# Low passes one image later, weight preparation over images 21 to 31, and a rearranged last stage

## The chip, the cores and the metric

The kernel runs on one NeuronCore of one Trainium2 chip. The time is device microseconds of one execution; the time before is the median of three runs. One further execution was profiled. Engines are named as the profile names them: PE (TensorE matmul; PEld its weight load), DVE (VectorE), ACT (ScalarE), POOL (GpSimd), SP (SyncE, which only issues DMAs here).

## The reference

Input x is 32 images of 128 channels and 32x32 pixels, float32.

```python
x = x + L0(_gn(x))     # _gn: group norm over 32 groups of 4 channels
x = x + L1(_gn(x))
# L0: xs = conv(x, w_i2s * mask, 1x3) + b_i2s       (taps 0 and 1 only, tap 1 masked)
#     for each of the 32 rows of an image:
#         hc = conv(h, w_s2s, 1x3 along the 1024 columns b*w) + b_s2s
#         i, f, g, o = split((x_row + hc) @ w_ih.T + b_ih + b_hh)
#         c = sigmoid(f) * c + sigmoid(i) * tanh(g);  h = sigmoid(o) * tanh(c)
# L1: y = conv(x, W * het_mask, 3x3, p=4) + sum(b, axis=1)
#     het_mask: all nine taps where (i - n) % 4 == 0, the centre tap elsewhere
```

## The kernel before

The program has three stages, one behind the other. Within a stage every engine runs a fixed list of instructions, written out in Python in the order in which they are issued, and semaphores tie the engines together. An instruction that waits holds back all that stands behind it on its engine.

**First stage: the input convolution, one image b = 0 to 31 per loop turn ("step b").** ACT normalizes the image (`norm_image`, L914, writes `xn`) and rounds it to float16 (`high_image`, L924, writes `hi`; for every fourth image, b % 4 == 0, POOL does this, L825). POOL forms the remainder `lo` (L827). PE then does for the image eight **high** matmuls (`input_high`, `wi_hi` and `wi_lo` on `hi`, two halves of the image) and four **low** matmuls (`input_low`, `wi_hi` on `lo`; the last one raises `xconv_done`). An image's result lies in PSUM until it is copied into `img` by `store_xs`: ACT does even images (L929) and DVE odd ones (L601), both two steps late (`EVAC_LAG = 2`), so ACT's store of image b-2 stands in its list behind the norm and the rounding of image b. Three images fit in PSUM and three in each of `xn`, `hi` and `lo`.

The group norm needs statistics. DVE takes them (`bn_stats`, L466, two instructions for an image), sums a chunk of up to four images (`bn_aggr`, L474), and a chain of small steps follows: PE `sum_means`, DVE `chain_mean`, PE `sum_vars`, DVE `chain_var`, ACT `square_root`, DVE `chain_rstd` (ends with `nbias`, L511). `CHAIN_AT` and `ROOT_AT` say at which step PE, DVE and ACT do their part. The sums for images 18 to 21 are at step 14, for 22 to 25 at step 18, for 26 to 29 at step 22 and for 30 and 31 at step 26; their roots are on ACT at steps 16, 20, 24 and 28, behind the norm of that step and ahead of its store.

In the same stage the weights are prepared: PE turns them by transposes (`turn` with `raw_s` and `raw_g`, `turn_conv` with `turn_c`), all three into one PSUM bank, and DVE splits each result into a high and a low half (`split`, L575 and L578; `split_conv`, L589 and L596). Since they share the bank, the next turn waits until the split before it is done (`split_done`). DVE's `top_weights` and `scale_weights` find the scale of the last convolution's weights, and one DVE instruction of 1152 columns (L648) scales them for all three rows of taps. `TURN_STATE`, `TURN_GATES`, `TURN_ROWS`, `TOP_AT`, `SCALE_AT` and `TURN_CONV_AT` name the steps.

**Second stage: the recurrence,** 96 items (32 rows times 3 column blocks); nothing of it is changed.

**Third stage: the last convolution, 16 groups g of two images.** ACT writes the normalized images into `pad` (L1016), DVE their low parts (`lo`, L729). Four classes of output channels q = 0 to 3 need different input channels, so POOL copies every `pad` twice into a `stack` (L883 for odd classes, L884 for even ones) and then shifts the even classes' rows (L888, two instructions); the odd ones' are shifted by two DMAs from SP (`stack_below`, L415). PE does for a group `dense` (L1249) and `tiled` (L1271) for each of three `TERMS`, then `residual` (L1259), then `above_and_below` (L1291, 144 matmuls that read the stacks), whose last matmul raises `conv_done`. ACT and DVE then finish two classes each (`finish_class`, L1035 and L735), and SP stores the group by four DMAs of 256 KB; of the last group's four, ACT issues two.

Of the kernel before, what the change touches and what calls it, by code (L numbers as in the profile page):

```python
# [19 lines left out]
Q = 4  # L20
# [64 lines left out]
ACT_CLASSES, DVE_CLASSES = (0, 2), (1, 3)  # L85

# [30 lines left out]
def build_network(nc, x, w_i2s, b_i2s, w_s2s, b_s2s, w_ih, b_ih, b_hh, w_conv, b_conv, consts, out):  # L117
# [4 lines left out]
    with ExitStack() as ctx:  # L122
# [138 lines left out]
        conv_done = sem("conv_done")  # L261
        class_set = sem("class_set")
# [109 lines left out]

        @block.sync
        def _(sp):
# [59 lines left out]
            for g in range(GROUPS):  # L434
                sp.wait_ge(out_act, len(ACT_CLASSES) * (g + 1))
                sp.wait_ge(out_dve, len(DVE_CLASSES) * (g + 1))
                store_group(sp, g, range(Q) if g < GROUPS - 1 else range(2))
                for b in range(PAIR * (g + 2), min(PAIR * (g + 3), B)):
                    stack_below(b)
            sp.wait_ge(stored, 16 * Q * GROUPS)  # L440
# [3 lines left out]
        def _(v):  # L444
# [140 lines left out]

            def split_conv(d):
# [35 lines left out]
            for b in range(B):  # L622
# [16 lines left out]
                if b == TURN_STATE + 1:  # L639
                    split(1, ws_hi, ws_lo)  # L640
# [6 lines left out]
                if b == TURN_CONV_AT:  # L647
                    v.tensor_scalar(turn_c[:].rearrange("p k (q n) -> p k q n", q=Q),  # L648
                                    raw_c[:].rearrange("p (n q) k -> p k q n", q=Q), scl[:, 5:6], None,
                                    ALU.mult).then_inc(raws_ready, 1)  # L650
                if b - 1 in TURN_ROWS:
                    split_conv(TURN_ROWS.index(b - 1))
            zlow(0)
# [77 lines left out]

            def finish_class(g, q):

                v.wait_ge(conv_done, g + 1)
# [34 lines left out]
            lo(2)  # L769
            image_stats_again(2 * CH - 1)  # L770
            bn_aggr(FIRST_CHUNKS + 2)
            lo(3)
            chain_mean(FIRST_CHUNKS + 2)
            image_stats_again(HELD)
            image_stats_again(HELD + 1)
            for g in range(GROUPS):
# [3 lines left out]
                finish_class(g, DVE_CLASSES[0])  # L780
                if chain:
                    chain_mean(FIRST_CHUNKS + k + 1)
                finish_class(g, DVE_CLASSES[1])
# [7 lines left out]
                if near < B:  # L791
                    lo(near)
                if chain:
                    chain_rstd(FIRST_CHUNKS + k + 1, (k + 1) % 2)
# [4 lines left out]
                if near < B:  # L799
                    lo(near + 1)  # L800

        @block.gpsimd
        def _(pool):
# [70 lines left out]
            for b in range(PAIR, B):  # L874
# [10 lines left out]
                pool.wait_ge(odd_stacked, b - PAIR + 1)  # L885
# [5 lines left out]
        def _(act):  # L891
# [40 lines left out]
            for q in QUARTERS[2:]:  # L932
                load_quarter(act, 0, q)
# [423 lines left out]
```

## Time and profile before

| what | value |
|---|---|
| median of three runs | 638.57 us (636.14 to 638.76) |
| the profiled execution's own time | 636.83 us |
| its span | 635.0 us |
| busy | PE 92%, DVE 80%, ACT 76%, POOL 64% |
| first stage | 0 to about 124 us |
| second stage | about 124 to 434 us |
| third stage | about 434 to 635 us |
| TensorE clock granted, whole run | 0.984 of full |

A busy share is an average over three stages with different limits. For this change only the first and the third stage are read: in each, the question is which wait of PE ends last, and what the engine that is waited for was doing before. A matmul's duration in the rows is modelled and overlaps the next one, so PE's pace is read from the distance between two starts.

### The profile page before, as it was taken

How to read it: one execution, taken by the hardware profiler on the slowest of the kernel's cores; microseconds unless marked ns; L12 is line 12 of the kernel's file. 1: busy time of each engine (PE TensorE's matmuls, PEld its weight loads, DVE VectorE, ACT ScalarE, POOL GpSimd, SP SyncE). 2: the span in 40 equal slices, each digit the busy share in tenths (PEclk: the TensorE clock that was granted, in tenths of full speed). 3: DMA queues.
4: the chain of work that ended last, by engine and by line, in shares of the span. 5: the costliest groups of instructions: out<-in, count | busy, mean ns of one | idle time of the engine just before them, and what ended most of it. 6: DMA issues, size and time to landing. Idle time of an engine off the chain costs nothing.

```text
span 635.0 us, 19609 instructions
## 1 busy us (share of the span) xinstructions
PE 581.3 (92%) x7741; PEld 382.4 (60%) x7741; DVE 507.3 (80%) x1187; ACT 485.8 (76%) x867; POOL 403.7 (64%) x373
## 2 busy tenths in 40 slices
PE   0889897999999999999999999995799999999995
PEld 0434444578888888878888888883444444343342
DVE  4887887489999999999999999997876786666430
ACT  1678884899999999989999999997373645536440
POOL 1478885545555555565555555554479999998891
PEclk9999997999999999999999999997899999999999
DMA  9978940004314444224443144400156465664745
GB/s 242 273 221 269 232 53 1 3 4 68 51 29 57 67 68 66 41 28 67 68 68 51 26 60 66 68 2 1 26 133 167 122 164 133 151 159 118 178 121 150
DMA packets 89659, 61.47 MB, mean 97 GB/s; under 512 B 73952, under 2 KB 75232, under 8 KB 89568
## 3 DMA queue, kind: packets, MB, share of 16 engines
q1 hardware_dynamic: 88608, 58.90, 44.4%
q10 hardware_dynamic: 960, 1.31, 0.7%
q8 instruction: 62, 1.02, 0.7%
q14 instruction: 29, 0.24, 0.1%
HBM read 35.07 MB, written 16.78 MB: 82 GB/s over the span
## 4 chain that ended last, share of the span: by engine, by line
PE 61%; POOL 17%; DVE 10%; ACT 5%; issue 4%; DMA 1%; SPq 0%; POOLq 0%; DVEq 0%; ACTq 0%
PE ps L1191 18%; PE ps L1169 13%; PE ps L1196 9%; POOL stack L888 8%; PE ps L1173 6%; POOL stack L884 5%; POOL stack L883 4%; PE ps L1291 3%; PE ps L1114 3%; PE ps L1115 3%; DVE bn L466 3%; PE ps L1249 2%; PE ps L1271 1%; ACT xn L914 1%; DMA img<-in_x_dram 1%
## 5 line engine op out<-in xcount | busy, mean ns | idle before, releaser
L846 POOL TENSOR_TENSOR fc<-gate,cell 128x352 f32<-128x352 f32 (+16 forms) x96 | 83.8, 873 | 141.6 <-ACT gate L975 141.6
L1191 PE MATMUL ps<-z_hi,wg_hi 128*128 128x352 f32 (+13 forms) x384 | 134.3, 351 | 1.2 <-ACT z_hi L959 0.8
L1191 PE MATMUL ps<-z_hi,wg_lo 128*128 128x352 f32 (+13 forms) x384 | 122.0, 319 | 0.0
L1196 PE MATMUL ps<-z_lo,wg_hi 128*128 128x352 f32 (+13 forms) x384 | 107.5, 320 | 0.0
L975 ACT ACTIVATE gate<-ps,gate_bias 128x352 f32<-128x352 f32 (+16 forms) x192 | 104.2, 543 | 2.9 <-PE ps L1196 2.9
L975 ACT ACTIVATE ps<-ps,gate_bias 128x352 f32<-128x352 f32 (+16 forms) x192 | 99.5, 518 | 0.0
L856 POOL TENSOR_TENSOR img<-hT,xr 128x352 f32<-128x352 f32 (+1 forms) x96 | 88.7, 924 | 5.8 <-DVE hT L693 5.6
L1035 ACT ACTIVATE img<-ps,finish 128x512 f32<-128x512 f32 x32 | 23.2, 774 | 89.1 <-PE ps L1291 81.0
L827 POOL TENSOR_TENSOR lo<-xn,hi 128x1024 f16<-128x1024 f32 x32 | 68.1, 2131 | 28.4 <-ACT hi L924 27.2
L466 DVE BATCH_NORM_STATS2 bn<-img 128x6 f32<-128x512 f32 x120 | 75.8, 681 | 7.6 <-DMA img<-in_x_dram 7.5
L1191 PEld LDWEIGHTS ps<-z_hi,wg_hi 128*128 128x128 f32 x384 | 72.3, 188 | 8.1 <-ACT z_hi L959 1.4
L1191 PEld LDWEIGHTS ps<-z_hi,wg_lo 128*128 128x128 f32 x384 | 72.5, 189 | 0.0
L1196 PEld LDWEIGHTS ps<-z_lo,wg_hi 128*128 128x128 f32 x384 | 68.2, 188 | 0.8 <-DVE z_lo L607 0.3
L888 POOL COPY stack<-pad 32x1074 f32<-32x1074 f32 x46 | 60.0, 1304 | 4.6 <-POOL stack L884 0.4
L672 DVE TENSOR_TENSOR hrow<-ps,tc 128x352 f32<-128x352 f32 (+16 forms) x96 | 49.2, 513 | 16.9 <-ACT tc L984 15.7
L735 DVE TENSOR_SCALAR img<-ps,finish 128x512 f32<-128x512 f32 x32 | 25.0, 806 | 45.5 <-PE ps L1291 44.9
L607 DVE SCALAR_TENSOR_TENSOR z_lo<-ps,z_unscale,z_hi 128x352 fp32r<-128x352 f32 (+15 forms) x96 | 54.9, 572 | 3.8 <-ACT z_hi L959 2.4
L1169 PE MATMUL ps<-hh,ws_hi 128*128 128x352 f16 (+19 forms) x279 | 56.7, 312 | 0.5 <-DVE hh L679 0.5
L1173 PE MATMUL ps<-hl,ws_hi 128*128 128x352 f16 (+19 forms) x279 | 55.7, 308 | 0.4 <-DVE hl L685 0.4
L1169 PE MATMUL ps<-hh,ws_lo 128*128 128x352 f16 (+19 forms) x279 | 55.7, 308 | 0.0
L1291 PE MATMUL ps<-stack,wk_hi 64*32 64x512 f16 x1440 | 47.8, 383 | 7.8 <-POOL stack L888 4.3
L959 ACT ACTIVATE z_hi<-ps,z_unscale 128x352 fp32r<-128x352 f32 (+15 forms) x96 | 52.4, 546 | 0.2
(141 smaller groups left out, 1309.8 us busy)
## 6 DMA issues: line engine op xcount, KB each, us to landing
xr<-in_x_dram SPq DMA_DIRECT2D x64, 256.0 KB, 5.5
img<-in_x_dram SPq DMA_DIRECT2D x126, 128.0 KB, 3.8
out_dram<-img SPq DMA_DIRECT2D x62, 256.0 KB, 4.2
stack<-pad SPq DMA_DIRECT2D x46, 134.2 KB, 2.5
stack<-pad_first SPq DMA_DIRECT2D x14, 134.2 KB, 3.0
raw_c<-in_L_conv_W_dram SPq DMA_DIRECT2D x4, 144.0 KB, 2.6
out_dram<-img ACTq DMA_DIRECT2D x2, 256.0 KB, 4.6
img<-in_x_dram ACTq DMA_DIRECT2D x2, 128.0 KB, 3.4
```

Source lines behind the costliest of these rows:

```text
L466: v.bn_stats(bn[:, j, s, :], src[:, 512 * s:512 * s + 512]).then_inc(bn_done, 1)
L607: v.scalar_tensor_tensor(out=z_lo[it % 2][:, 0:n], in0=z_even(it), scalar=z_unscale[:], in1=z_hi[it % 2][:, 0:n].bitcast(F32), op0=ALU.mul ...
L827: pool.tensor_tensor(lo0[slot][:], xn0[slot][:], hi0[slot][:], ALU.subtract).then_inc(lo0_done, 1)
L846: pool.tensor_tensor(fc[it % 2][:, 0:c1 - c0], gate[it % 2][0][:, 0:c1 - c0], cell[:, c0:c1], ALU.mult).then_inc(fc_done, 1)
L856: pool.tensor_tensor(img32[:, b0:b1, t, :], hT[it % 2][:, 0:W * (b1 - b0)].rearrange("p (b w) -> p b w", w=W), xr[:, r % 2, b0:b1, t % 2, ...
L888: pool.tensor_copy(below(b, q).bitcast(F32), rows_below(b, q).bitcast(F32)).then_inc(even_below, 1)
L975: act.activation(gate[it % 2][m][:, 0:n] if m in (0, 2) else gate_columns(it, m), gate_columns(it, m), ACT.Tanh if gt == G_GATE else ACT.S ...
L1169: pe.matmul(z, w[:, tap, :], hh[u][:, c0 + tap:c1 + tap], start=False, stop=False, skip_group_check=True)
L1173: ins = pe.matmul(z, ws_hi[:, tap, :], hl[u][:, c0 + tap:c1 + tap], start=False, stop=(tap == 2), skip_group_check=True)
L1191: pe.matmul(gbank(it, m)[:, 0:n], w[:, GATE_ORDER[m], :], z_hi[it % 2][:, 0:n], start=(w is wg_hi), stop=False)
L1196: pe.matmul(gbank(it, m)[:, 0:n], wg_hi[:, GATE_ORDER[m], :], z_lo[it % 2][:, 0:n], start=False, stop=True).then_inc(gate_ready, 1)
L1291: ins = pe.matmul(rows(out_rows(g, 2 * half + k, c)), WK[w][r, k, e], pixels.rearrange("p (h w) -> p h w", w=PADW)[:, :, 0:W], start=False ...
```

## The change

1. **First stage, low passes.** At step b PE does the high passes of image b and then the low passes of image b-1. Step 0 has no low passes, step 31 has those of images 30 and 31. `xconv_done` of an image is thus raised one step later in PE's list; no other engine's list is moved for that.
2. **First stage, weights.** The turn of `raw_s` goes from step 0 to step 21, its split from step 1 to step 23; the turn of `raw_g` from 22 to 23, its split from 23 to 24; `top_weights` from 22 and 23 to 25 and 26; `scale_weights` from 24 to 27. The single DVE instruction of 1152 columns becomes three of 384, at the ends of steps 28, 29 and 30 (`turn_row`), and `turn_conv` on PE goes from steps 26, 28, 30 to 28, 29, 30, each waiting for its own `turn_row`.
3. **Start.** ACT loads its function table (the `Sqrt` on `warm`) before it issues the DMAs of `raw_i`, `raw_s`, `mask` and `ident`, not behind them.
4. **Third stage, copies.** The copy of `pad` for the odd classes goes from POOL to DVE (`stack_odds`), behind each `lo`.
5. **Third stage, order on PE.** In groups 1 to 14 the residual and the stack matmuls of the first two terms come before the dense and tiled matmuls of the third term; only the third term's stack matmuls stay last.
6. **Last group.** The stack matmuls of the even classes come first and raise `evens_done`; each of ACT and DVE finishes one even class, then one odd class; the stores are split in even and odd classes of 128 KB, eight DMAs in all, of which six lie on SP and two on ACT.

```diff
-TURN_STATE, TURN_GATES, TURN_ROWS = 0, 22, (26, 28, 30)
+TURN_STATE, TURN_GATES, TURN_ROWS = 21, 23, (28, 29, 30)
-BIAS_AT, TOP_AT, SCALE_AT, TURN_CONV_AT = 16, (22, 23), 24, 25
+BIAS_AT, TOP_AT, SCALE_AT = 16, (25, 26), 27
...
+            def turn_row(d):
+                k = slice(3 * d, 3 * d + 3)
+                v.tensor_scalar(turn_c[:, k].rearrange("p k (q n) -> p k q n", q=Q),
+                                raw_c[:].rearrange("p (n q) k -> p k q n", q=Q)[:, k], scl[:, 5:6], None,
+                                ALU.mult).then_inc(raws_ready, 1)
...
-                if b == TURN_STATE + 1:
+                if b == TURN_STATE + EVAC_LAG:
                     split(1, ws_hi, ws_lo)
...
-                if b == TURN_CONV_AT:
-                    v.tensor_scalar(turn_c[:]...
                 if b - 1 in TURN_ROWS:
                     split_conv(TURN_ROWS.index(b - 1))
+                if b in TURN_ROWS:
+                    turn_row(TURN_ROWS.index(b))
...
+            def stack_odds(b):
+                v.wait_ge(lo_done, b + 1)
+                if b >= PAIR + SLOTS:
+                    v.wait_ge(conv_done, (b - SLOTS) // PAIR + 1)
+                v.tensor_copy(stack[b % SLOTS][1][:].bitcast(F32), pad[b % SLOTS][:].bitcast(F32)).then_inc(odd_stacked, 1)
...
-                evens, odds = stack[b % SLOTS]
-                pool.tensor_copy(odds[:].bitcast(F32), pad[b % SLOTS][:].bitcast(F32)).then_inc(odd_stacked, 1)
-                pool.tensor_copy(evens[:].bitcast(F32), pad[b % SLOTS][:].bitcast(F32)).then_inc(even_stacked, 1)
+                pool.tensor_copy(stack[b % SLOTS][0][:].bitcast(F32), pad[b % SLOTS][:].bitcast(F32)).then_inc(even_stacked, 1)
...
-                pe.wait_ge(raws_ready, 3)
+                pe.wait_ge(raws_ready, 3 + d)
...
                 input_high(b, 1)
-                input_low(b)
+                if b > 0:
+                    input_low(b - 1)
+                if b == B - 1:
+                    input_low(b)
...
+                if g < GROUPS - 1:
+                    residual(g)
+                    stacks_ready(g)
+                    above_and_below(g, TERMS[:2], (0, 1), False)
+                    dense(g, TERMS[2:], False)
+                    tiled(g, TERMS[2:], SIDES, False)
+                    above_and_below(g, TERMS[2:], (0, 1), True).then_inc(conv_done, 1)
+                else:
+                    dense(g, TERMS[2:], False)
+                    tiled(g, TERMS[2:], SIDES, False)
+                    residual(g)
+                    stacks_ready(g)
+                    above_and_below(g, TERMS, (0,), True).then_inc(evens_done, 1)
+                    above_and_below(g, TERMS, (1,), True).then_inc(conv_done, 1)
```

How the order moves on PE around step 22. `hi00`, `lo00` are the slots of image 21 (21 % 3 = 0), `hi01`, `lo01` those of image 22, `hi02` that of image 23 (and 20). Before, from the low passes of image 21 on:

```order
L1114 MATMUL ps<-lo00,wi_hi 128x512 [waits lo0_done]
L1115 MATMUL ps<-lo00,wi_hi 128x16x31
L1114 MATMUL ps<-lo00,wi_hi 128x512
L1115 MATMUL ps<-lo00,wi_hi 128x16x31
L1082 MATMUL ps<-mv,group_mean 128x4 [waits aggr_done]
L1091 MATMUL ps<-ident,raw_g 128x128 [waits split_done,par_in]
L1091 MATMUL ps<-ident,raw_g 128x128 x3
L1114 MATMUL ps<-hi01,wi_hi 128x512 [waits xs_odd_done,hi0_done]
```

And now, from the second half of image 22's high passes on:

```order
L1149 MATMUL ps<-hi01,wi_hi 128x512 [waits xs_odd_done,hi0_done]
L1150 MATMUL ps<-hi01,wi_hi 128x16x31
L1149 MATMUL ps<-hi01,wi_lo 128x512
L1150 MATMUL ps<-hi01,wi_lo 128x16x31
L1149 MATMUL ps<-lo00,wi_hi 128x512 [waits lo0_done]
L1150 MATMUL ps<-lo00,wi_hi 128x16x31
L1149 MATMUL ps<-lo00,wi_hi 128x512
L1150 MATMUL ps<-lo00,wi_hi 128x16x31
L1126 MATMUL ps<-ident,raw_g 128x128 [waits split_done,par_in]
L1126 MATMUL ps<-ident,raw_g 128x128 x3
L1149 MATMUL ps<-hi02,wi_hi 128x512 [waits xs_even_done,hi0_done]
```

The low passes of image 21 are now the last thing ahead of the turn of `raw_g`, and this turn waits for `split_done` of `raw_s`.

DVE at the same place, now: the end of the chain of step 22, the store of image 21, statistics of image 31, and the splits.

```order
L526 SCALAR_TENSOR_TENSOR nbias0<-ps,rstd0 128x4 [waits gn_step]
L623 COPY img<-ps 128x1024 [waits xconv_done]
L481 BN_STATS bn<-img 128x6 [waits x_in7]
L481 BN_STATS bn<-img 128x6
L590 CAST ws_hi<-ps 128x384 [waits prep_T]
L593 TENSOR_TENSOR ws_lo<-ps,ws_hi 128x384 [waits prep_hi]
L598 COPY wgT<-ps 128x512 [waits prep_T]
```

The split of `raw_s` (`ws_hi`, `ws_lo`) stood some 170 rows further up before, at step 1; now it stands behind a store that waits for the low passes of image 21.

POOL in the third stage, one image before:

```order
L883 COPY stack21<-pad2 128x1107
L884 COPY stack20<-pad2 128x1107
L888 COPY stack20<-pad2 32x1074 x2
```

and now:

```order
L917 COPY stack30<-pad3 128x1107
L920 COPY stack30<-pad3 32x1074 x2
```

The full copy for the odd classes has left POOL; DVE has it behind its `lo`.

## Rows read from the trace of the kernel before

**Rows 1.** Ten microseconds: length, busy (instructions) of PE, PEld, DVE, ACT, POOL; clock, DMA

```profile
100.00:110.00 10.00, 6.54 (x24) 4.29 (x25) 5.62 (x18) 1.45 (x3) 5.24 (x3) 0.66 0.01 2
```

**Rows 2.** Timeline, PE: start, length, engine, line, instruction, [idle before <-releaser]

```profile
96.68 0.38 PE L1114 MATMUL ps<-hi,wi_hi 128*128 128x512 f16 x1
...
99.05 0.38 PE L1115 MATMUL ps<-lo,wi_hi 128*128 128x496 f16 x1
101.72 0.38 PE L1082 MATMUL ps<-mv,group_mean 128*128 128x2 f32 x2 [2.29 <-DVE mv L474]
103.85 0.90 PE L1099 MATMUL ps<-ident,turn_c 128*128 128x128 f32 x3 [1.75 <-DVE turn_c L648]
...
106.49 0.63 PE L1115 MATMUL ps<-hi,wi_hi 128*128 128x496 f16 x1
106.92 0.63 PE L1114 MATMUL ps<-hi,wi_lo 128*128 128x512 f16 x1
...
124.23 0.38 PE L1115 MATMUL ps<-lo,wi_hi 128*128 128x496 f16 x1
```

**Rows 3.** Timeline, ACT in the first stage: images 10 to 14, and 22

```profile
49.95 1.24 ACT L914 ACTIVATE xn<-img,nbias,rstd 128x1024 f32<-128x1024 f32 x1 [1.12 <-DVE nbias L511]
...
54.35 1.06 ACT L924 ACTIVATE hi<-xn 128x1024 f16<-128x1024 f32 x1
55.32 1.23 ACT L914 ACTIVATE xn<-img,nbias,rstd 128x1024 f32<-128x1024 f32 x1
56.45 1.00 ACT L929 ACTIVATE img<-ps 128x1024 f32<-128x1024 f32 x1
...
61.05 1.24 ACT L914 ACTIVATE xn<-img,nbias,rstd 128x1024 f32<-128x1024 f32 x1 [1.12 <-DVE nbias L511]
...
83.57 1.23 ACT L914 ACTIVATE xn<-img,nbias,rstd 128x1024 f32<-128x1024 f32 x1
```

**Rows 4.** Waits over the span: who waited for whom, us, times, longest

```profile
PE ps L1291 <- POOL stack L888: 4.3, 8, 0.8
```

**Rows 5.** Timeline, ACT and its DMA queue at the end of the run

```profile
627.40 1.45 ACT L1035 ACTIVATE img<-ps,finish 128x512 f32<-128x512 f32 x2 [8.91 <-PE ps L1291]
629.02 1.80 ACTq L369 DMA_DIRECT2D out_dram<-img  x2
```

**Rows 6.** Timeline, PE: first stage, steps 1 and 14

```profile
25.08 0.38 PE L1082 MATMUL ps<-mv,group_mean 128*128 128x3 f32 x2 [0.41 <-DVE mv L474]
...
66.40 0.39 PE L1082 MATMUL ps<-mv,group_mean 128*128 128x4 f32 x2 [1.81 <-DVE mv L474]
```

**Rows 7.** Timeline, PE: the start of group 1 in the third stage

```profile
454.15 0.39 PE L1082 MATMUL ps<-mv,group_mean 128*128 128x4 f32 x2 [2.54 <-DVE mv L474]
...
455.54 0.64 PE L1249 MATMUL ps<-pad_first,wall_hi 128*32 128x512 f16 x2
```

**Rows 8.** Timeline, DVE: steps 21 to 27 of the first stage

```profile
92.72 1.23 DVE L601 COPY img<-ps 128x1024 f32<-128x1024 f32 x1
93.97 1.29 DVE L466 BATCH_NORM_STATS2 bn<-img 128x6 f32<-128x512 f32 x2
95.29 0.93 DVE L553 TENSOR_REDUCE cand<-raw_c 32x1 f32<-32x288 f32 x2
...
96.57 0.52 DVE L559 TENSOR_SCALAR class_finish<-class_of,conv_bias 128x4 f32<-128x4 f32 x1
...
98.93 0.15 DVE L564 TENSOR_REDUCE top<-cand 128x1 f32<-128x2 f32 x1
...
100.26 1.22 DVE L601 COPY img<-ps 128x1024 f32<-128x1024 f32 x1
...
101.58 2.21 DVE L648 TENSOR_SCALAR turn_c<-raw_c,scl 128x1152 f32<-128x1152 f32 x1
...
110.74 0.55 DVE L589 CAST wall_hi<-ps 128x384 f16<-128x384 f32 x1
```

**Rows 9.** Groups of instructions, DVE, 200 to 280 us: busy us, mean ns

```profile
L679 DVE TENSOR_SCALAR hh<-hrow 128x352 f16<-128x352 f32 (+16 forms) x25 | 8.3, 331 | 0.0
```

More of the change, by code:

```diff
@@ L371, in store_group, with store_last @@
                                  .rearrange("p (q x) -> p q x", q=Q)).then_inc(stored, 16)
+        def store_last(engine, classes, pieces):
+            g = GROUPS - 1
+            for c in pieces:
+                r = slice(32 * c, 32 * c + 32)
+                b, row = piece(g, c)
+                engine.dma_start(out_q[classes[0]::2, :, b, W * row:W * row + PIECE].rearrange("q n x -> n q x"),
+                                 img32[r, PAIR * g:PAIR * g + PAIR].rearrange("p b h w -> p (b h w)")
+                                 .rearrange("p (q x) -> p q x", q=Q)[:, classes[0]::2]).then_inc(stored, 16)
         @block.sync
@@ L792, in _ @@
                     lo(near)
+                    stack_odds(near)
                 if chain:
@@ L800, in _ @@
                     lo(near + 1)
+                    stack_odds(near + 1)
         @block.gpsimd
@@ L1032, in finish_class @@
             def finish_class(g, q):
-                act.wait_ge(conv_done, g + 1)
+                if g == GROUPS - 1 and q in EVEN:
+                    act.wait_ge(evens_done, 1)
+                else:
+                    act.wait_ge(conv_done, g + 1)
                 act.activation(group_out(g, q), y_bank(g, q), ACT.Identity, bias=finish[:, 0, q:q + 1],
@@ L1072, in _ @@
             act.wait_ge(out_dve, len(DVE_CLASSES) * GROUPS)
[L1073 removed]
+            store_last(act, ODD, range(2, Q))
         @block.tensor
@@ L1281, in above_and_below @@
                 pe.wait_ge(even_below, len(EVEN) * (PAIR * g))
-                for m, (w, part) in enumerate(TERMS):
+            def above_and_below(g, terms, parities, last):
+                for m, (w, part) in enumerate(terms):
                     for e in range(3):
-                        for k in range(2):
+                        for k in parities:
                             for c in range(Q):
@@ L1292, in above_and_below @@
                                                     pixels.rearrange("p (h w) -> p h w", w=PADW)[:, :, 0:W], start=False,
-                                                    stop=m == len(TERMS) - 1 and e == 2, tile_position=(64 * half, 32 * c),
-                                                    skip_group_check=True)
-                ins.then_inc(conv_done, 1)
+                                                    stop=last and m == len(terms) - 1 and e == 2,
+                                                    tile_position=(64 * half, 32 * c), skip_group_check=True)
+                return ins
             pe.wait_ge(split_done, 3 + 3)
@@ L1319, in _ @@
                 pe.wait_ge(lo_done, PAIR * (g + 1))
-                for m in range(len(TERMS)):
+                for m in range(2):
                     dense(g, TERMS[m:m + 1], m == 0)
```

38 lines of the change are left out of this document (21 added, 17 removed).

## The prediction

> **Forecast:** slower, 658 us against a median of 638.57. The third stage gains some 5 us; the first loses several times that, because what the low passes and the weights are moved behind is exactly what other engines wait for.
>
> **What bounds the kernel now.** I read the stages one by one. In the third, PE's starts follow each other almost without a hole; the waits view gives PE 4.3 us of waiting in eight places for POOL's shifted copies [rows 4]. After PE's last matmul come two finishes on ACT, a DMA issue of 1.8 us and the landing: from 627.4 to 635.0 [rows 5]. The second stage is not touched. In the first stage PE's own work on an image is twelve matmuls, from 96.68 to 99.05 + 0.22 = 99.27, so 2.59 us [rows 2]. The one large hole is at image 26: idle 2.29 and 1.75 us, and then matmuls 0.43 us apart instead of 0.216 [rows 2]; in this stretch the granted clock averages 0.66 [rows 1], a mix of 2.4 and 1.2 GHz. But PE is not the only full engine. From image 10 to image 14 ACT takes 61.05 - 49.95 = 11.10 us [rows 3] where PE needs 4 x 2.59 + 0.28 = 10.65: ACT leads there and spends 1.12 us of it waiting for `nbias`. So what the reader is to look for is not PE's holes alone, but how much room ACT's list has.
>
> **Part 1: low passes behind the next high ones.** ACT's store of image b-2 waits for the low passes of b-2. These now come after the high passes of b-1, which need ACT's rounding of b-1. Take image 11: `hi` ends at 54.35 + 1.06 = 55.41. PE then needs 1.73 us of high passes, 0.86 of low ones and about 0.2 until the result is seen, so the store of image 10 starts at 58.2. Before, ACT put only the norm of 12 in between and stored at 56.45 [rows 3]. That is 1.8 us of new waiting in each group of four images, in ACT's list, with nothing behind it able to pass.
> - Images 6 to 14, where ACT leads: 2 x 1.8 = **+3.6**.
> - Images 14 to 22. At step 14 PE waits for DVE's statistics until 66.40, with 1.81 us idle [rows 6]. It now arrives after the low passes of 12 and not of 13, and ACT is later by no less than DVE, so it is idle about 3.9. DVE's work is unchanged. The low passes of 14 then stand behind those of 13 and the high ones of 15: ACT's store of 14 falls at 13.3 us after the norm of 14 began if the clock has dropped (11.0 if not), where it was 8.6. I carry that to the norm of 18: 16.5 us after that of 14 (14.1 if not). The next four, paced by ACT, rounding and both stores with PE's 2.8 us in between, take 12.05. Sum 28.5 against 83.57 - 61.05 = 22.5 [rows 3]: **+6.0** (+3.6 with the clock up).
> - Step 1. Ahead of the sums at 25.08 [rows 6] PE had four low passes, then 0.43 us apart, and three transposes, nearly 3 us in all; now it is idle that long. It ran at the low clock so far. If that lasts over step 1, the low passes of 0 end at 31.0 and ACT's list, which stores image 0 behind them, is 3 us later by image 6; if not, nothing is lost. I take the middle, **+1.5**, and keep 0 and 3.
>
> **Part 2: the weights.** With ACT's norm of image 22 as zero (83.57 in the trace), and durations from [rows 8]: store 1.15, an image's statistics 1.25, a split of 384 columns 2 x 0.55, `top_weights` second part 96.97 - 95.29 = 1.7, `scale_weights` 100.26 - 98.93 = 1.33, `turn_row` 2.21 / 3 = 0.75.
> - Step 23. PE finishes the low passes of 21 at 6.1. Then it wants the turn of `raw_g`, which waits for the split of `raw_s`. DVE is still in the chain of step 22: it waits for the root that ACT takes behind the norm of 24, at 7.3, ends the chain at 8.4, stores 21 (9.6), takes statistics (10.85) and splits (12.0). PE is idle 5.9 us.
> - PE's clock is low for some 5.7 us after such a hole: after 103.85 it was until 110 [rows 2]. High passes of 23 to 16.3, low of 22 to 17.9. ACT: store 22, norm and rounding of 25 to 21.3; PE: 25, low passes of 24 to 24.0. Sums of 26 are ready by then. ACT: store 24, norm and rounding of 27 to 27.35, norm of 28, root 28.6; PE is through step 27 at 30.0.
> - Step 28. `turn_conv` waits for `turn_row`. DVE from the root at 28.6: chain 1.0, `top_weights` 1.7, store of 25 1.15, `scale_weights` 1.33, `turn_row` 0.8: 34.6. PE is idle 4.6 us, turns and makes the gate bias at the low clock (2.3, as from 103.85 to 106.1), and the step ends at 41.2.
> - Step 29. DVE's list is store of 27 (which needs the low passes of 27, PE's last work in step 28), `split_conv`, `turn_row`: 3.3 us in which PE is idle, since the second `turn_conv` waits for it. 44.5; with the rest of the step at a partly low clock 49.1.
> - Steps 30 and 31 and the last low passes: 56.0. Before, 124.23 + 0.22 - 83.57 = 40.9 [rows 2, 3]: **+15.1**. The hole at image 26 is gone within this, and three others stand in its place. Were the clock high throughout, 48.7: +7.8.
>
> The rule that speaks against this change: the Trainium skill, page TensorE: Matmul & The Clock Gate, Part 1: The HAM clock gate (the "warmup" mystery), says that the default is throttled and activity releases it. The trace agrees, at 0.66. By the rule each new hole is paid twice, and the sum is the one above; without it, it is the first rival.
>
> What shows in the trace itself: behind a hole of 2.54 us in the third stage the matmuls of 455.54 take 0.64 us [rows 7], like those of the low clock in rows 2. The new holes, of 3.3 to 5.9 us, are longer.
>
> **Part 3: the start.** The DMAs of four parameter tiles are issued 1.5 us later and leave the queues to image 1. The statistics of image 1 waited for its load; I take **-0.4** (0 to -0.9). The parameters are needed only behind those.
>
> First stage: 1.5 + 3.6 + 6.0 + 15.1 - 0.4 = **+25.8**; with the clock high, and the other ends, 14.1; at most 27.7.
>
> **Part 4: the third stage.** POOL loses 1.1 us an image, and PE's waits for it, 4.3 in the view and nearly 5.0 between starts, can go [rows 4]. The new order asks for the stacks 1.6 us earlier, for which POOL's 2.2 us a group suffice; what is late next is DVE, which gets two copies of 1107 columns a group. Its like (one operand and result in SBUF, 352 columns) takes 0.33 [rows 9], which makes 0.7; the slow bound is 1.2, as for 1024 columns in [rows 8]. `lo` of the second image is then ready 9.5 us after `conv_done`, and PE asks for it at 10.3. I take -3.5 (-1 to -5), short of the whole since PE's holes marked "issue" may appear where POOL's wait hid them. At the start of group 1 PE waits for DVE's statistics [rows 7], and one copy now stands ahead: +0.7 (0.3 to 1.2). The tail: one finish instead of two behind the last matmul (-0.7), and 128 KB a DMA with half the issue time behind it: together -2.4 (-1.5 to -2.8). Sum **-5.2** (-2.0 to -7.3).
>
> **The sum** goes against the profiled execution's own 636.83: 636.8 + 25.8 - 5.2 = 657.4. The median of the runs shown lies 1.7 above that execution; I add 0.6 for it: **658**.
>
> **The rivals.**
> - *The clock stays at 2.4 GHz over the new holes.* 636.8 + 14.1 + 0.5 - 5.2 = 646. For it: nothing in the trace has a hole of this length in the midst of the first stage. Against: shorter ones [rows 2, 7] did it. Chance 0.18.
> - *ACT's store is not on the path:* PE lags behind ACT so far that the low passes are the later thing anyway, and only the three holes of part 2 count: 636.8 + 15.1 + 1.1 - 5.2 = 648. For it: up to 99.05 PE ran for some images without a hole. Against: rows 3. Chance 0.12.
> - *The other side: faster.* DVE has split `raw_s` and scaled a row before PE asks; then the hole of image 26 goes (99.27 to 106.1, less 1.2 of necessary turns, plus 1.8 of slow matmuls: 7.4) and nothing replaces it: 636.8 - 7.4 - 5.2 = 624. It is decided at step 23: DVE's `ws_lo` must end before PE's low passes of 21. Against it stands the order itself, since DVE's store in front of it waits for those passes. Chance 0.04.
> - *The two stages cancel,* with half of the first stage's losses absorbed: 637 to 641. Chance 0.06.
>
> **Chances and range.** The forecast has 0.6. Faster by over 0.5% (about what a measurement of this kernel can tell from no change) has 0.05, within it 0.05, slower 0.9. The range 643 to 664 takes in the low sum (636.8 + 14.1 - 7.3 = 643.6) with its two slow rivals, and the high one (636.8 + 27.7 - 2.0 = 662.5).
>
> **What would show it.** Right: PE idle 5 to 6 us before the turn of `raw_g`, waiting for `ws_lo`; 4 to 5 before the first `turn_conv` and 3 before the second; ACT's stores waiting for PE once or twice in four images; the first stage ending near 150 instead of 124.5; PE's wait for POOL in the third stage near zero. Wrong: a first stage under 138, or a hole that is not there, or a third stage that isn't shorter by 3 us. Most doubtful is how much of ACT's 1.8 us per four images adds up once PE, and not ACT, is late.

## The result, and the profile after

| | before | changed |
|---|---|---|
| median of four executions, us | 637.73 | 664.48 |
| lowest and highest, us | 636.14 to 638.76 | 662.12 to 665.44 |
| profiled execution, us | 636.83 | 662.12 |
| its span, us | 635.0 | 660.3 |
| end of the first stage (start of the last low pass), us | 124.23 | 152.62 |

The changed kernel is slower: the ratio is 1.041, with a 95% interval from 1.039 to 1.044. The forecast was 658 us in a range of 643 to 664, so the direction and the place were right, and the size was 6.5 us too small, just outside the range. The median of before is 637.73 here, and not the 638.57 that the forecast names, because a fourth execution is counted. The profiled execution of the changed kernel is the lowest of its four: 662.12 lies inside the range, the median outside.

Up to the end of the first stage 28.4 us are lost (forecast 25.8); behind it 3.1 are won (forecast 5.2). PE's three holes are there, and the longer one at step 14 too. In PE's timeline after, the bracket is the idle time ahead and its releaser (compare [rows 2, 6]):

```profile
72.84 0.59 PE L1117 MATMUL ps<-mv,group_mean 128*128 128x4 f32 x2 [3.74 <-DVE mv L489]
...
107.61 1.08 PE L1126 MATMUL ps<-ident,raw_g 128*128 128x128 f32 x4 [5.37 <-DVE ws_lo L593]
108.49 0.63 PE L1149 MATMUL ps<-hi,wi_hi 128*128 128x512 f16 x1
...
110.51 0.38 PE L1150 MATMUL ps<-hi,wi_hi 128*128 128x496 f16 x1
...
131.01 0.90 PE L1134 MATMUL ps<-ident,turn_c 128*128 128x128 f32 x3 [6.63 <-DVE turn_c L604]
...
141.37 0.90 PE L1134 MATMUL ps<-ident,turn_c 128*128 128x128 f32 x3 [3.17 <-DVE turn_c L604]
...
152.62 0.38 PE L1150 MATMUL ps<-lo,wi_hi 128*128 128x496 f16 x1
```

The waits of the first stage (14 to 155 us; us in total, times, longest) say that the other engines wait too, for PE's low passes:

```profile
ACT img L961 <- PE ps L1150: 34.6, 12, 9.2
DVE img L623 <- PE ps L1150: 22.1, 8, 7.3
PE ps L1134 <- DVE turn_c L604: 9.8, 2, 6.6
PE ps L1126 <- DVE ws_lo L593: 5.4, 1, 5.4
```

These waits are circular: ACT and DVE wait with a store for the low passes, and PE waits for what DVE does behind its store. In ACT's timeline (compare [rows 3]) a cycle of four images is now 67.50 - 53.79 = 13.71 us, where it was 11.10:

```profile
53.79 1.24 ACT L946 ACTIVATE xn<-img,nbias,rstd 128x1024 f32<-128x1024 f32 x1 [1.12 <-DVE nbias L526]
...
63.05 1.02 ACT L961 ACTIVATE img<-ps 128x1024 f32<-128x1024 f32 x1 [2.67 <-PE ps L1150]
...
67.50 1.24 ACT L946 ACTIVATE xn<-img,nbias,rstd 128x1024 f32<-128x1024 f32 x1 [1.12 <-DVE nbias L526]
...
95.57 1.23 ACT L946 ACTIVATE xn<-img,nbias,rstd 128x1024 f32<-128x1024 f32 x1
```

What the forecast did not have is in DVE's timeline ahead of the hole of step 28:

```profile
125.15 1.91 DVE L574 TENSOR_SCALAR class_finish<-class_of,conv_bias 128x4 f32<-128x4 f32 x1
...
128.47 0.15 DVE L553 TENSOR_SCALAR scl<-top 128x1 int32<-128x1 int32 x1
...
129.10 0.92 DVE L583 TENSOR_SCALAR ident_y<-ident,scl 128x128 f32<-128x128 f32 x1
...
130.07 0.88 DVE L604 TENSOR_SCALAR turn_c<-raw_c,scl 128x384 f32<-128x384 f32 x1
```

POOL's timeline beside it:

```profile
124.92 2.12 POOL L862 TENSOR_TENSOR lo<-xn,hi 128x1024 f16<-128x1024 f32 x1
127.82 2.12 POOL L862 TENSOR_TENSOR lo<-xn,hi 128x1024 f16<-128x1024 f32 x1 [0.78 <-ACT hi L956]
```

`class_finish` had taken 0.52 us [rows 8], and this was already the end of such a wait: it ended at 97.09, and POOL's `lo` beside it at 97.07.

```profile
94.94 2.13 POOL L827 TENSOR_TENSOR lo<-xn,hi 128x1024 f16<-128x1024 f32 x1 [0.44 <-ACT hi L924]
```

Now it takes 1.91 and ends at 127.06, when POOL's `lo` of 124.92 ends (127.04); `ident_y` ends at 130.02, just behind the next `lo` (129.94). The small 128x1 instructions between run beside that `lo` in 0.15.

### The profile page after: what moved, and what is told of

It is laid out like the page before. It is cut to its first block, busy times and chain, and to the rows that moved or that the text cites. A ratio compares the mean times of both kernels' runs of the same rounds, so it can differ in the third digit from the quotient of the medians.

```text
span 660.3 us, 19612 instructions
## 1 busy us (share of the span) xinstructions
PE 590.4 (89%) x7741; PEld 379.8 (58%) x7741; DVE 535.5 (81%) x1219; ACT 485.9 (74%) x867; POOL 375.7 (57%) x343
## 4 chain that ended last, share of the span: by engine, by line
PE 73%; SPq 9%; DVE 8%; ACT 5%; issue 3%; DMA 0%; DVEq 0%; ACTq 0%
PE ps L1229 17%; PE ps L1207 12%; PE ps L1332 9%; PE ps L1234 9%; SPq L310 7%; PE ps L1287 6%; PE ps L1211 6%; PE ps L1309 4%; PE ps L1149 3%; PE ps L1150 2%; PE ps L1297 2%; DVE bn L481 2%; ACT xn L946 2%; ACT hi L956 1%; DVE img L623 1%
## 5 line engine op out<-in xcount | busy, mean ns | idle before, releaser
L692 DVE TENSOR_TENSOR hrow<-ps,tc 128x352 f32<-128x352 f32 (+16 forms) x96 | 49.1, 513 | 16.9 <-ACT tc L1016 16.2
L920 POOL COPY stack<-pad 32x1074 f32<-32x1074 f32 x46 | 58.1, 1264 | 2.8
L1016 ACT ACTIVATE tc<-cell 128x352 f32<-128x352 f32 (+16 forms) x96 | 47.0, 489 | 6.7 <-DVE cell L686 2.9
L713 DVE STREAM_TRANSPOSE hT<-hrow 128x352 f32<-128x352 f32 (+1 forms) x96 | 50.3, 524 | 0.0
```

Source lines behind the costliest of these rows:

```text
L920: pool.tensor_copy(below(b, q).bitcast(F32), rows_below(b, q).bitcast(F32)).then_inc(even_below, 1)
```

## Experiments

**Which edit costs what.** Four kernels (the changed one and three runs) share the changed third stage and start, and differ in the two edits of the first stage.

`a1_low_at_once` (PE, in the loop over the images):

```
-                if b > 0:
-                    input_low(b - 1)
-                if b == B - 1:
-                    input_low(b)
+                input_low(b)
```

> The changed kernel with the low passes of image b back behind its own high ones; weights and third stage as changed. Theory A (the two edits of the first stage cost apart from each other): DVE's list around the three turns is what is late, with or without the shift of the low passes, so PE stays idle some 4 to 6 us before the turn of raw_g and before the first turn_conv and 2 to 3 before the second. Only the longer cycles up to image 22 (12 us) and little more go: 664.5 - 12 - 2 = about 650. Theory B (the holes come of both edits together, since DVE's stores in front of the splits wait for the shifted passes): the holes go too, and the time falls under that of the kernel before, to 627 to 632.

`a3_low_behind_only` keeps the shift of the low passes and has the weights' schedule of the kernel before, with its split of `raw_s` in step 1 and its one scaling instruction of 1152 columns:

```
-TURN_STATE, TURN_GATES, TURN_ROWS = 21, 23, (28, 29, 30)
-BIAS_AT, TOP_AT, SCALE_AT = 16, (25, 26), 27
+TURN_STATE, TURN_GATES, TURN_ROWS = 0, 22, (26, 28, 30)
+BIAS_AT, TOP_AT, SCALE_AT, TURN_CONV_AT = 16, (22, 23), 24, 25
```

> The changed kernel with the weights' schedule of the kernel before; low passes one image later, third stage as changed. Theory A: 12 us are lost up to image 22 as in the changed kernel, and some 2 more behind it, where the hole of image 26 is there again: 634 + 14 = 648. Theory B: the same 12 up to image 22; behind it the hole of image 26 grows by the store that waits, 2 to 4 us: 650.

`a2_third_stage_only` has both of these edits.

> The kernel before with the third stage and the start as changed; low passes and weights as before. Both theories: the first stage ends at 124 as before, and the third is 3.5 us shorter, which with 0.3 at the start makes 637.7 - 3.8 = 634. If the third stage's gain hung on where the first one left the clock or the queues, it would be 637 to 638.

| weights \ low passes | at once | one image later |
|---|---|---|
| as before | 633.8 (a2); last low pass 124.07 | 653.2 (a3); 139.40 |
| images 21 to 31 | 638.9 (a1); 129.39 | 664.5 (changed); 152.62 |

Neither theory had it. The shift alone costs 19.4 us, the weights alone 5.1, and together they cost 6.2 more than the sum (at the last low pass 15.3, 5.3 and 7.9). The trace of a3 explains 15.3 of the 19.4 only: its profiled execution took 649.8, 3.4 less than its median, and where the others lose the rest isn't shown. Theory A was wrong on the size (it had 650 for a1): without the shift the holes of steps 23 and 28 are still there, at 4 us each, but the third isn't. The holes add up to 8.0 us, where the changed kernel has 15.2:

```profile
95.91 0.63 PE L1126 MATMUL ps<-ident,raw_g 128*128 128x128 f32 x4 [3.96 <-DVE ws_lo L593]
96.38 0.38 PE L1149 MATMUL ps<-hi,wi_hi 128*128 128x512 f16 x1
...
113.92 0.55 PE L1134 MATMUL ps<-ident,turn_c 128*128 128x128 f32 x3 [4.05 <-DVE turn_c L604]
```

Those two holes replace the one of image 26 of the kernel before, so that the net is only 5. a2 came out as expected. It is 0.994 of before, interval 0.9925 to 0.996: the rearranged third stage, with the new start, is a gain of about 4 us.

**Where the two edits meet.** `b2_behind_to_21` puts the low passes behind their own high ones from image 22 on:

```
-                if b > 0:
+                if 0 < b <= LOW_TO + 1:
                     input_low(b - 1)
-                if b == B - 1:
+                if b > LOW_TO:
                     input_low(b)
```

with LOW_TO = 21.

> The changed kernel, but from image 22 on the low passes stand behind their own high ones. Up to image 22 all is as in the changed kernel (ACT's norm of 22 near 95.6). Theory: the low passes of 27 are done in step 27 and not in step 28, so DVE's store in front of split_conv doesn't wait and the third hole goes; the holes at steps 23 and 28 shrink from 5.4 and 6.6 to the 4.0 and 4.1 of the run without any shift. From the norm of 22 to the end of the first stage 45 to 47 us where it was 57: 654. Rival: the holes grew because of the state in which images 6 to 21 leave ACT and DVE, not by the shift itself: the stretch stays at 54 or more, 662.

650.9, where 654 was expected. ACT is as late at image 22 as in the changed kernel (96.34), and from there to the last low pass it takes 45.5 us instead of 57.1. The rival falls: the shift behind image 22 is what makes the stretch longer. The third hole is gone and the others are near those of a1:

```profile
108.36 0.83 PE L1127 MATMUL ps<-ident,raw_g 128*128 128x128 f32 x4 [4.51 <-DVE ws_lo L594]
...
128.05 0.55 PE L1135 MATMUL ps<-ident,turn_c 128*128 128x128 f32 x3 [4.05 <-DVE turn_c L605]
```

**The first images.** `b1_behind_from_6` does the same the other way round (`input_low(b)` up to image 5, `input_low(b - 1)` from image 7 on).

> The changed kernel, but the low passes of images 0 to 5 stand behind their own high ones; from image 6 on they are one image later. ACT's norm of image 6 starts at 40.16 in the changed kernel and at 37.65 with the low passes at once. Theory: the 2.5 us go straight through, since ACT's list leads from there on: 662; and if step 1 is also where the timed executions lose more than the profiled one (664.5 against 662.1), 660. Rival: they are absorbed by the waits for DVE's statistics of images 14 to 17: 664.5.

662.1. ACT's norm of 6 starts at 37.32, 2.8 us earlier, that of 22 at 93.52, 2.1 earlier, and the last low pass 1.3 earlier. The median, 2.4 lower, is what the theory had, but in the traces a half is absorbed on the way to the last low pass. Behind it this profiled execution (662.8) is 2.0 us slower than that of the changed kernel, for which I have no row.

**What the clock costs.** `b3_holes_filled`:

```
+                if b in FILL:
+                    pe.wait_ge(hi0_done, b + 1)
+                    if b >= CONV_SLOTS:
+                        xs_stored(pe, b - CONV_SLOTS)
+                    for _ in range(FILL[b]):
+                        pe.matmul(rows(x_banks(b)[:, 0, :]), wi_hi[:, 1, :], rows(hi0[b % CONV_SLOTS][:])[:, 0:H // 2],
+                                  start=True, stop=True)
```

with FILL = {1: 7, 14: 13, 23: 23}.

> The changed kernel with needless matmuls of 512 columns in PE's holes: 7 ahead of the sums of step 1, 13 ahead of those of step 14, 23 ahead of the turn of raw_g in step 23 (they write a bank that the image's first matmul overwrites; the outputs are the same). Nothing that PE waits for changes, only the clock. Theory (each long hole is paid again by a low clock behind it): the matmuls right behind the three holes take 0.216 and not 0.43 us, ACT's stores behind them come earlier, and the first stage ends some 5 us sooner: 660. Rival (the low clock lies beside other waits): 664.

The median is 659.3, or 5.2 less, as expected. The traces give less: the last low pass starts at 150.62, 2.0 earlier than in the changed kernel and 3.8 earlier than in its second profile (f1, below). PE's rows at step 23 are those of a high clock; the turn waits only 0.41:

```profile
106.47 0.63 PE L1127 MATMUL ps<-ident,raw_g 128*128 128x128 f32 x4 [0.41 <-DVE ws_lo L594]
106.93 0.38 PE L1150 MATMUL ps<-hi,wi_hi 128*128 128x512 f16 x1
```

The stages name the shares: from ACT's norm of 14 to that of 22 26.5 us instead of 28.1 (1.5 less), from there to that of 25 16.2 instead of 17.6 (1.4 less). The seven at step 1 came too late: PE had already been idle 2.59 us ahead of them, and they took 2.93 us together, so the clock was low when they began. The profiled executions differ by 3.0 only; the other two microseconds of the medians have no row.

**Why the hole of step 28 was 6.6 us.** `e1_class_finish_by_columns`:

```
-                    v.tensor_scalar(class_finish[:, 0], class_of[:], conv_bias[:], None, ALU.mult).then_inc(bias_ready, 1)
+                    for q in range(Q):
+                        v.tensor_scalar(class_finish[:, 0, q:q + 1], class_of[:, q:q + 1], conv_bias[:], None,
+                                        ALU.mult).then_inc(bias_ready, 1)
...
-                    pe.wait_ge(bias_ready, 2)
+                    pe.wait_ge(bias_ready, 1 + Q)
```

> The changed kernel, but DVE's class_finish of 128x4 in top_weights is computed in four instructions of 128x1. In the changed kernel it took 1.91 us (0.52 in the kernel before) and ended with POOL's lo that ran beside it, while DVE's 128x1 instructions of the scale ran 0.15 each beside the next one. Theory (the form with four columns waits until POOL's instruction is over, the one with one column doesn't): 4 x 0.15 = 0.6 us instead of 1.9, the hole of step 28 is 5.3 instead of 6.6 us, the whole 663. Rival (whatever comes there on DVE waits for POOL): no change.

The median is 661.8, but the profiled execution is as long as that of the changed kernel (662.2 against 662.1), and the hole is 6.53, where the theory had 5.3. The trace shows why. DVE:

```profile
125.40 0.58 DVE L575 TENSOR_SCALAR class_finish<-class_of,conv_bias 128x1 f32<-128x1 f32 x4
...
128.02 0.29 DVE L585 TENSOR_SCALAR ident_y<-ident,scl 128x128 f32<-128x128 f32 x1
128.22 2.09 DVE L587 TENSOR_SCALAR class_finish<-class_of,y_unscale 128x4 f32<-128x4 f32 x1
130.23 0.87 DVE L606 TENSOR_SCALAR turn_c<-raw_c,scl 128x384 f32<-128x384 f32 x1
```

POOL:

```profile
125.17 2.13 POOL L864 TENSOR_TENSOR lo<-xn,hi 128x1024 f16<-128x1024 f32 x1
128.07 2.22 POOL L864 TENSOR_TENSOR lo<-xn,hi 128x1024 f16<-128x1024 f32 x1 [0.78 <-ACT hi L958]
```

The first `class_finish` no longer waits (0.58). But `ident_y`, 1.1 us earlier, now slips in ahead of POOL's `lo` of 128.07, and the second `class_finish` of 128x4, which had taken 0.22, meets it and takes 2.09. The wait moved to the next instruction of the kind.

`g1_no_wait_for_pool` takes the rest out of the way too: `ident_y` and the second `class_finish` stand behind the first `turn_row`.

```
                 v.wait_ge(scales_ready, 1)
 
+            def scale_rest():
+
                 v.tensor_scalar(ident_y[:], ident[:], scl[:, 5:6], ACT_SCALE, ALU.mult, ALU.mult).then_inc(ident_scaled, 1)
...
                 if b in TURN_ROWS:
                     turn_row(TURN_ROWS.index(b))
+                if b == TURN_ROWS[0]:
+                    scale_rest()
```

> The changed kernel with class_finish of top_weights by columns (4 x 0.15 us) and with ident_y and the second class_finish behind the first turn_row instead of in front of it. Theory (DVE's instructions that end with POOL's are the 2 us by which the hole of step 28 was larger than forecast): it goes from 6.6 to 4.2 us, 1.3 from the first and 1.1 from the second, and the first stage ends 2 to 3 us earlier: 661. Rival: turn_row itself waits for POOL's lo in its turn and takes up to 2 us: hole 6 or more, 663.5.

661.7. The hole is 4.36, the last low pass starts at 150.08 instead of 152.62. `turn_row`, whose operand is read with a stride, isn't held up beside the `lo` of 128.15, and `ident_y` behind it is, until 130.36. These waits are not all of the difference between the holes: in a1 and b2, whose holes are 4.05, `class_finish` took 1.92 us as well. PE at the turn:

```profile
129.06 0.90 PE L1140 MATMUL ps<-ident,turn_c 128*128 128x128 f32 x3 [4.36 <-DVE turn_c L608]
```

DVE ahead of it:

```profile
128.10 0.91 DVE L608 TENSOR_SCALAR turn_c<-raw_c,scl 128x384 f32<-128x384 f32 x1
128.92 1.44 DVE L587 TENSOR_SCALAR ident_y<-ident,scl 128x128 f32<-128x128 f32 x1
```

**The copies of the third stage.** `a4_odds_on_pool` gives both copies back to POOL (it drops the calls of `stack_odds` on DVE and restores the line `pool.tensor_copy(odds, pad)` of the kernel before).

> The changed kernel with both copies of the shifted rows on POOL again; PE's new order and the tail kept. If DVE's copies cost what POOL's waits cost before, the time stays within 1 us of 664.5. If the copies off POOL are what gained, PE waits for POOL again, and sooner than before since the new order asks for the stacks 1.6 us earlier: 4 to 8 us more, 668 to 672. If the DVE copy costs more than it gives (it takes 1.50 us beside a POOL copy, not 0.7): 662.

666.3, between the first and the second expectation. The copies on DVE are worth about 2 us: 1.8 in the medians, whose intervals overlap (1.0428 to 1.0483 of before, against 1.0389 to 1.0437), and 2.5 behind the last low pass in the profiled executions; the other 0.6 by which the spans differ lie in the first stage, which is the same. PE doesn't wait for POOL here, but 2.4 us for the DMAs of the shifted rows behind POOL's copies.

**Schedules without the holes.** The weights' work is done as early as before, but row by row. `c1_weights_early_low_at_once`, against the changed kernel:

```
-TURN_STATE, TURN_GATES, TURN_ROWS = 21, 23, (28, 29, 30)
-BIAS_AT, TOP_AT, SCALE_AT = 16, (25, 26), 27
+TURN_STATE, TURN_GATES, TURN_ROWS = 0, 22, (28, 29, 30)
+BIAS_AT, TOP_AT, SCALE_AT, ROWS_BY = 16, (22, 23), 24, (26, 27, 28)
```

with `input_low(b)` at once, the split of `raw_s` in step 1 and `turn_row` on DVE in the steps of ROWS_BY; `c2_weights_early_low_behind` has the same with the shift.

> Both edits of the first stage mended: low passes at once; raw_s turned and split at the start as in the kernel before, top_weights and scale_weights at 22 to 24 as there, but the three turn_rows one by one in steps 26 to 28 and the three turn_convs in steps 28 to 30. Theory (what is late in every hole is DVE's list, and 2.2 us of turn_conv in one piece made the hole of image 26): no hole over 1 us from image 22 on, first stage 6 to 7 us shorter than the 124 of the kernel before: 627. Rival: the DVE work is merely late elsewhere, 633 to 634.

> The weights' schedule of the run with no hole behind image 26 (raw_s turned and split at the start, top_weights at 22 and 23, scale_weights at 24, turn_rows in steps 26 to 28, turn_convs in steps 28 to 30), with the low passes one image later as in the changed kernel. Theory: the holes of steps 23 and 28 go, that of step 29 stays at about 3 us, since DVE's store of 27 in front of split_conv waits for the low passes: about 648. Rival (the shift alone makes DVE late enough that the turns wait whatever their order): 653 or more.

c1 takes 629.8 (0.989 of before, interval 0.987 to 0.992), better than both kernels, but not the 627 of the theory: the first stage is 3.4 us shorter than before and not 6 to 7 (last low pass 120.80), and one hole over 1 us is left, ahead of the sums of step 26. c2 takes 651.1, between the theory and the rival: the holes of steps 23 and 28 are gone, that of step 29 is 2.47, but the one ahead of the sums of step 26, which I had not counted, is 3.47. In c1 it is 2.28:

```profile
101.38 0.38 PE L1117 MATMUL ps<-mv,group_mean 128*128 128x2 f32 x2 [2.28 <-DVE mv L489]
```

`d1_scale_behind_chain_26` sets TOP_AT = (22, 26) and SCALE_AT = 26. `g3_scale_26_no_wait_for_pool` sets TOP_AT = (22, 23) and SCALE_AT = 26, and has the two edits of g1.

> Low passes at once, raw_s split at the start, third stage as changed, turn_rows in steps 26 to 28 and turn_convs in 28 to 30, but top_weights' second part and scale_weights in step 26, behind the chain of that step. Theory (the hole of 2.28 us ahead of the sums of step 26 is the 3 us of this work in front of the statistics): the hole goes with its low clock, 3 to 3.5 us less than 629.8: 626.5. Rival: the first turn_row is then late for step 28, a hole of 2 to 4 us there as in the run with top_weights at 25 and 26, 630 or more.

> Low passes at once, raw_s split at the start, third stage as changed, top_weights at 22 and 23, scale_weights in step 26 behind the chain, class_finish by columns, ident_y and the second class_finish behind the first turn_row. Theory: 1.3 us of DVE's work go from in front of the sums of step 26, so the hole of 2.28 there becomes 1.0, and turn_row is 1 to 2 us earlier than with top_weights in step 26 too, so the 4.05 of step 28 become 0.5 or less: no low clock behind either, first stage near 118, 627 against the 629.8 of the best so far. Rival: a hole of 1 us here and one there cost as much as one of 2.3: 630.

d1: 632.4; the rival came true. The hole of step 26 is gone and one of 4.05 stands at step 28: `class_finish` took 1.92 us and `ident_y` 1.52, beside POOL. g3: 629.9, the rival's number. The hole of step 26 is the 1.0 forecast and that of step 28 is gone; one of 0.93, which I had not counted, stands at step 29. The rival's reason isn't borne out: from ACT's norm of 22 to the last low pass it takes 1.8 us less than c1 (35.7 against 37.6), but the whole isn't shorter. PE, g3:

```profile
101.41 0.38 PE L1123 MATMUL ps<-mv,group_mean 128*128 128x2 f32 x2 [1.01 <-DVE mv L489]
...
111.90 0.52 PE L1140 MATMUL ps<-ident,turn_c 128*128 128x128 f32 x3 [0.93 <-DVE wall_lo L622]
```

In the profiled execution 1.6 of the 1.8 went to the clock at step 14; whether they did so in the others isn't shown. Four microseconds behind the same hole of 1.80 us (length, busy time of PE, PEld, DVE, ACT, POOL, clock, DMA share, GB/s), in c1:

```profile
66.00:70.00 4.00, 3.94 (x21) 1.95 (x21) 3.04 (x14) 2.17 (x4) 3.58 (x3) 1.00 0.86 278
```

And in g3:

```profile
66.00:70.00 4.00, 4.00 (x15) 1.61 (x14) 3.42 (x14) 1.14 (x2) 3.92 (x3) 0.65 0.98 275
```

ACT's norm of 18 starts 11.8 us behind that of 14 in c1, in a2 and in the kernel before, and 13.3 to 13.4 in g3, d1 and a1, though the list is the same. Which of c1 and g3 is faster stays open.

**The changed kernel again.**

> The changed kernel again. Its profiled execution took 662.1, its timed ones 664.0 to 665.4. If the two differ in the first stage, step 1 or one of the three holes is longer here; if in the second or third, the first stage ends near 152.8 again and the stages behind it are 2 us longer.

663.5, ratio 1.041 again. Its first stage has the same holes (5.37, 6.63, 3.17) and is 1.8 us longer, of which 1.0 is there at ACT's norm of 6: behind step 1's hole PE's matmuls stay 0.43 us apart until 30.1 and not until 28.2. This is read from their starts; the granted clock in the view of this execution is 1.00 there, which doesn't fit them.

## Why the prediction was off

The mechanism held. What failed are the sizes of four terms of the sum. The store's wait was priced at 1.8 us and is 2.67, twice (+1.6). The hole of step 28 was priced at 4.6 and is 6.63 (+2.0). Groups 1 to 15 of the third stage were to gain 3.5 and gained 1.6 (+1.9). And 0.6 was added for the median, which lies 2.4 above the profiled execution (+1.8). Errors the other way gave back about 1. The first stage's 28.4 us lie above even the 27.7 that I called the most.

By its own terms, in the profiled executions (span 635.0 to 660.3, +25.3, where 20.6 was forecast):

| term | forecast | measured |
|---|---|---|
| start and step 1, to ACT's norm of 6 | +1.1 | +1.3 |
| ACT's store waits, images 6 to 14 | +3.6 | +5.2 |
| images 14 to 22 | +6.0 | +5.5 |
| weights, norm of 22 to the last low pass | +15.1 | +16.4 |
| third stage | -5.2 | -3.1 |

The rest is the median: it lies 2.4 above the profiled execution here, and I had added 0.6; f1 shows the clock at step 1 as one source.

- **The start and step 1: right by luck.** I took the middle between 0 and 3. From ACT's norm of 0 to that of 6 it is 24.47 us against 22.86, so +1.6, because the clock rose in the midst of the stretch; in f1, where it rose later, it is +2.6.

- **The two cycles: right mechanism, term too small.** I priced the store's wait at 1.8; it is 2.67. Of the difference 0.48 is a wait that I left out of PE's step 11: the sum of variances (60.88) waits for DVE, whose chain begins at 60.20, behind its own store of 59.06. The two sums themselves take PE 0.25 us each in that step. a3, with the weights as before, has the same waits (2.59 and 2.67), so they come from the shift alone.
- **Step 23: right.** PE's turn of `raw_g` starts 12.0 us behind ACT's norm of 22, as forecast.
- **Step 28: mis-sized by 2.** Forecast 4.6, measured 6.6. DVE's list from the root to the end of `turn_row` took 8.2 us (122.8 to 130.95) where I had 6.0. I took each DVE instruction at its length in [rows 8], and two of them fell beside POOL's `lo`: 2.0 of the 2.2. g1, without these two waits, has 4.36.
- **Step 29: right** (3.3 forecast, 3.17 measured), and its cause too: b2 removes it by letting the low passes of 27 be done in step 27.
- **The clock: too dear at step 23.** I let it be low for 5.7 us behind step 23's hole; it was for 2.6 (107.61 to 110.2), and b3 gives back 1.4 there, where my step had 3. Behind step 28's hole it stayed low for 6.5 us (131.0 to 137.5), where I had the same 5.7. The error of step 23 made PE ready for step 28 1.2 us sooner than forecast and cancels a part of that of step 28, which is why part 2 as a whole came out within 1.3. In b3 the filled holes of steps 14 and 23 keep the granted clock at 1.00. The rule of the Trainium skill, page TensorE: Matmul & The Clock Gate, Part 1: The HAM clock gate (the "warmup" mystery), that activity releases the throttle, agrees with this. But a hole of 3.96 us in a1 left the matmuls behind it at full speed, so not every long hole is paid twice, which the forecast had assumed.
- **The third stage: short by 2.1.** PE's waits for POOL are gone and the tail is 2.0 shorter (forecast 2.4). The +0.7 for a longer wait for DVE's statistics ahead of group 1 isn't there: this wait is 2.67 against 2.54 [rows 7], and the finish of group 0 comes as long behind the last low pass as before (334.9 against 335.0 us). The finish of group 0 to that of group 1 grew by 0.7, but it lies behind that wait, and a2 and b1, with the same third stage, have 10.64 and 10.62 there, less than the 10.97 of before: the number is luck. Groups 1 to 15 gained 1.6 and not 3.5. ACT's finishes, before:

```profile
459.24 1.45 ACT L1035 ACTIVATE img<-ps,finish 128x512 f32<-128x512 f32 x2 [8.10 <-PE ps L1271]
470.21 1.45 ACT L1035 ACTIVATE img<-ps,finish 128x512 f32<-128x512 f32 x2 [3.44 <-PE ps L1291]
```

After:

```profile
487.51 1.45 ACT L1070 ACTIVATE img<-ps,finish 128x512 f32<-128x512 f32 x2 [7.28 <-PE ps L1309]
499.15 1.45 ACT L1070 ACTIVATE img<-ps,finish 128x512 f32<-128x512 f32 x2 [1.78 <-PE ps L1332]
...
654.73 0.78 ACT L1070 ACTIVATE img<-ps,finish 128x512 f32<-128x512 f32 x1 [1.23 <-PE ps L1332]
```

PE's holes alone gave more than I forecast. Between the finishes of groups 1 and 14 (length, busy time of PE, PEld, DVE, ACT, POOL, clock, DMA share, GB/s), before:

```profile
470.10:616.90 146.80, 138.60 (x4191) 60.97 (x4184) 95.82 (x178) 78.18 (x84) 135.44 (x106) 1.00 0.59 146
```

After:

```profile
499.00:643.20 144.20, 140.71 (x4191) 57.65 (x4184) 119.46 (x206) 78.34 (x84) 111.00 (x80) 1.00 0.61 149
```

PE is idle 3.5 us there and not 8.2, but for the same 4191 matmuls it is busy 2.1 us longer. f1, a2 and a4 have 140.42, 140.74 and 141.11. a4 has POOL's copies back, so it isn't the copies. What the four share and the kernel before lacks is PE's new order, which I had put at no cost; no run takes back the order alone, so this is argued and not shown. From the finish of group 14 to that of 15 it is 1.0 longer (0.5 in f1).

One microsecond of the holes that are left is a new wait. In group 2 PE waits 0.97 for DVE's `lo`. Ahead of it in DVE's list stand copies that began at 485.40 and 496.40. My price for a copy, 0.7, holds for the second; the first fell among POOL's copies and took 1.50. DVE:

```profile
485.40 1.50 DVE L758 COPY stack<-pad 128x1107 f32<-128x1107 f32 x1
...
496.40 0.74 DVE L758 COPY stack<-pad_first 128x1107 f32<-128x1107 f32 x1
```

PE:

```profile
500.37 0.40 PE L1287 MATMUL ps<-pad_first,wall_hi 128*32 128x512 f16 x2 [0.97 <-DVE pad L749]
```

- **The rivals.** The one by which ACT's store isn't on the path falls with a3: the shift alone costs 15 us of the first stage, though it adds no work. The rival of the clock falls for the changed kernel: in both of its profiles PE's matmuls are 0.43 us apart behind the holes of steps 1, 14, 23, 28 and 29. What it had right is that the price at step 23 was too high.
- **Slips in the working.** The ends of part 4 don't add up to -2.0 and -7.3 but to -1.3 and -7.5. With these ends, 27.7 and the 1.7 by which the median lay above the profiled execution the high sum is 664.9, and the measured 664.48 lies below it; the range had left the median out. The 96.97 in `top_weights` stands in no row (the next instruction begins at 97.01). And the stretch of low clock behind 103.85, which I carried on as 5.7 us, is 6.1 in the rows (to 109.9).

## What to carry to other kernels

When work is moved behind another engine's next item, list what every other engine has queued behind the result: here two stores waited for the low passes, and behind DVE's store stood what PE needed next, so the two edits cost 6 us more together than apart. A long piece of work broken into rows gains while the rows stay early (c1, 629.8 against 633.8) and loses when it and what it waits for are moved to just before its use (a1, 638.9). A length in a row can hold a part of a wait, and it changes with the place: 0.52 us for `class_finish` was already more than the 0.22 of its twin, and became 1.91. Look at what POOL will be doing at the new place.

## What the runs showed of the hardware

- Some DVE instructions cannot start, or cannot end, beside POOL: 128x4 and 128x128 `tensor_scalar` from and to SBUF took 0.52 to 2.09 us when they met POOL's `tensor_tensor` of 2.13, as long as was left of it, and ended with it, against 0.22 and 0.29 alone. Beside the same instruction a 128x1 form took 0.15 and the strided `turn_row` 0.91, so it isn't every instruction on DVE. The Trainium skill, page Trainium Architecture — The Big Picture, section What this means for kernel authors, calls the shared port of these two engines "an exclusive lock (not a bandwidth split)"; the traces agree, with 1.91 us for four columns.
- The granted clock behind one and the same hole (1.80 us at step 14) fell in three profiled executions and not in three others, at a price of 1.6 us. Behind a hole of 3.96 us it stayed up once; behind the one of 3.73 or 3.74 at step 14 it fell in all nine profiled executions that have it, and behind one of 5.37 in all six.
